# Moving the second batch's first query projection and the first batch's inverse roots in a gated attention and expert kernel

## The reference

```python
x = x + tanh(g_xattn[0]) * xattn(layernorm(x), ctx_2048, Wq, Wk, Wv, Wsk, Wsv, Wo)
x = x + tanh(g_ffn[0]) * ffn(layernorm(x), router, gate, up, down, ...)
```

## Time and profile before

| | |
|---|---|
| median of 3 runs | 894.11 us (891.49 to 894.21) |
| profiled execution | 890.82 us |
| span of the profiled execution | 889.0 us |
| mean granted TensorE clock | 0.994 |
| PE busy | 870.7 us, 98% of the span |
| DVE, POOL, ACT busy | 539.9, 512.7, 398.7 us |

### The profile page before, as it was taken

One profiled execution on the slowest core, in us unless ns is written; L12 is line 12 of the kernel. 1 busy time (PEld: TensorE's weight loads), 2 busy tenths in 40 slices (PEclk: granted clock), 3 DMA queues, 4 the chain that ended last, 5 costly groups with the idle time before them and its releaser, 6 DMA issues.

```text
span 889.0 us, 17360 instructions
## 1 busy us (share of the span) xinstructions
PE 870.7 (98%) x6662; PEld 759.7 (85%) x6662; DVE 539.9 (61%) x977; ACT 398.7 (45%) x806; POOL 512.7 (58%) x532
## 2 busy tenths in 40 slices
PE   8899999999999999899999999999999999999998
PEld 8799999999999998778888867888888888888886
DVE  6566667666666656732246758466565565566567
ACT  5535555454555554654135143443444444444431
POOL 4824343434344322361579995456788888788741
PEclk9989999999999999999999999999999999999999
DMA  8558676767676563880101155402202010121046
GB/s 269 137 165 215 169 195 185 208 167 208 168 208 177 164 177 93 184 289 1 48 25 46 55 167 162 166 24 71 72 25 95 25 71 24 72 72 48 1 134 245
DMA packets 78099, 111.74 MB, mean 126 GB/s; under 512 B 7097, under 2 KB 48826, under 8 KB 76986
## 3 DMA queue, kind: packets, MB, share of 16 engines
q1 hardware_dynamic: 75808, 109.61, 42.2%
q10 hardware_dynamic: 2210, 1.03, 0.5%
HBM read 73.33 MB, written 33.62 MB: 120 GB/s over the span
## 4 chain that ended last, share of the span: by engine, by line
PE 91%; DVE 3%; DMA 2%; POOL 1%; issue 1%; ACT 1%; SPq 0%; POOLq 0%; DVEq 0%
PE ps_scores L2112 20%; PE ps_proj L1763 14%; PE ps_scoresT L2112 10%; PE ps_scoresT L1900 6%; PE ps_scores L1752 6%; PE ps_proj L1752 6%; PE ps_o L1914 6%; PE ps_scores L1873 5%; PE ps_scoresT L1752 5%; PE ps_proj L2112 5%; PE ps_proj L1821 4%; DMA q_kept<-second_qT_hi 1%; DMA xn_rows<-in_x 1%; PE ps_o_max L1932 1%; DVE neg_max L1406 1%
## 5 line engine op out<-in xcount | busy, mean ns | idle before, releaser
L1078 ACT ACTIVATE probsT<-ps_scoresT 128x512 f32<-128x512 f32 (+1 forms) x256 | 138.0, 544 | 148.9 <-PE ps_scoresT L1900 144.8
L1406 DVE TENSOR_REDUCE neg_max<-ps_scores 128x2 f32<-128x384 f32 (+1 forms) x256 | 131.0, 516 | 109.0 <-PE ps_scores L1873 108.3
L1288 ACT ACTIVATE part_sums<-ps_scores 128x512 f32<-128x512 f32 x96 | 57.4, 598 | 133.0 <-PE ps_scores L2112 130.2
L1900 PE MATMUL ps_scoresT<-q_stack,k_stack 116*128 116x256 f32 x448 | 106.3, 309 | 1.7 <-ACT probsT L1078 1.6
L1873 PE MATMUL ps_scores<-k_stack,q_stack 114*128 114x192 f32 (+1 forms) x512 | 96.9, 273 | 8.1 <-DVE neg_max L1406 7.9
L1873 PEld LDWEIGHTS ps_scores<-k_stack,q_stack 114*128 114x128 f32 x512 | 83.0, 194 | 14.8 <-DVE neg_max L1406 8.4
L807 POOL TENSOR_TENSOR o_normal<-o_blocks,inv_sums 128x256 f32<-128x256 f32 x32 | 19.9, 622 | 124.8 <-DVE inv_sums L1427 124.8
L950 POOL TENSOR_TENSOR w_expert_lo<-w_sums,w_expert_hi 128x256 fp32r<-128x256 f32 x64 | 63.8, 1008 | 45.5 <-ACT w_expert_hi L1211 45.5
L962 POOL TENSOR_TENSOR big<-big,basis 128x512 f32<-128x512 f32 x56 | 77.5, 1401 | 15.6 <-DVE basis L1702 15.6
L1900 PEld LDWEIGHTS ps_scoresT<-q_stack,k_stack 116*128 116x128 f32 x448 | 70.0, 190 | 6.3 <-ACT probsT L1078 2.8
L1693 DVE TENSOR_TENSOR basis<-part_sums,silu_gate 128x512 f32<-128x512 f32 x32 | 24.0, 750 | 67.3 <-ACT silu_gate L1296 67.3
(11 more groups left out here) (296 smaller groups left out, 2496.6 us busy)
## 6 DMA issues: line engine op xcount, KB each, us to landing
k_stack<-k_kept SPq DMA_DIRECT2D x64, 192.0 KB, 4.4
q_stack<-q_kept SPq DMA_DIRECT2D x48, 192.0 KB, 4.3
big<-coeff_rows SPq DMA_DIRECT2D x8, 1024.0 KB, 4.7
q_kept<-qT_hi SPq DMA_DIRECT2D x10, 512.0 KB
x_rows<-in_x SPq DMA_DIRECT2D x9, 512.0 KB, 5.4
k_kept<-kT_hi SPq DMA_DIRECT2D x16, 256.0 KB
x_kept<-x_rows SPq DMA_DIRECT2D x16, 256.0 KB, 3.5
w_raw<-in_L_ffn_w_gate SPq DMA_DIRECT2D x16, 256.0 KB, 2.9
```

The costliest lines, as they stand in the source:

```text
L1078: act.activation(PT[:, g % 2, 2 * j:2 * j + blocks].rearrange("p h f r w -> p (h f r w)"), ST[:, n % 2, 0:blocks].rearrange("p h n -> p (h ...
L1288: act.activation(TP[:, u % 2, j, :], src[:, u % 2, :], ACT.Copy).then_inc(taken, 1)
L1406: dve.tensor_reduce(NM[:, g // 2 % 2, g % 2, 2 * i:2 * i + 2], SA[:, n % 2, :, 0:keys], AX.X, ALU.max, negate=True).then_inc(max_done, 1)
L1900: ins = pe.matmul(ST[:, n % 2, v, :], KS[0:ROWS, g, j + v, 1 - v].rearrange("p w s -> p (w s)"), QS[0:ROWS, g, j + v].rearrange("p f r w - ...
```

## The change

Two things are done. First, the query (1, 0): its first half stays in the prologue; the second half of 12 matmuls is cut into four pieces of 3, which go behind the scores of slots 1, 3, 5 and 7. The other three queries of batch 1 move from slots 1 to 14 to slots 9 to 15. Since splitting is tied to the last part, ACT and DVE split the query (1, 0) in slot 8, not in slot 0, and the last of the four in slot 16, not 15; `keep_q(1)` stands in slot 17, not 16, of SP's program.

Second, the inverse roots of batch 0: DVE adds the epsilon (`first_variance`), ACT takes the square root (`first_sqrt`), DVE makes the reciprocal and the Newton step (`first_roots`); POOL no longer does it and starts with `rows_out(1)`. ACT gets two dummy activations of one column (`table_of`) that load the tables of the square root at the start and of the exponential behind the last `rows_out`. DVE splits the weight halves 4 and 5 later, around the normalisation.

```diff
-EARLY_Q = ((-1, -1, -1), (1, 4, 7), (9, 10, 11), (12, 13, 14))
+EARLY_Q = ((-1, -1, 7), (9, 10, 11), (11, 12, 13), (13, 14, 15))
+EARLY_PIECES = {1: 4, 3: 5, 5: 6, 7: 7}
...
         def x_roots(b):
-            pool.wait_ge(stats_done, TB * (b + 1))
+            pool.wait_ge(stats_done, TB * (b + 1) + 1)
             inverse_roots(mv, ve, rstd, tmp, b).then_inc(rstd_done, 1)
...
-        link(pool.memset(half[:], -0.5))
-        x_roots(0)
+        pool.memset(half[:], -0.5).then_inc(ones_set, 1)
+        pool.wait_ge(ones_set, 3)
         rows_out(1)
         x_roots(1)
...
+        def first_sqrt():
+            act.wait_ge(stats_done, TB + 1)
+            act.activation(rstd[:, 0:TB], ve[:, 0:TB], ACT.Sqrt).then_inc(rstd_done, 1)
+
+        def table_of(func):
+            act.activation(tg[:, 0:1], VA[:, 0, 0, 0:1], func)
...
+        act.wait_ge(ones_set, 1)
+        table_of(ACT.Sqrt)
         weights_high(0)
...
-        for n in range(1, 8):
+        for n in range(1, 5):
+            weights_high(n)
+        first_sqrt()
+        for n in range(5, 8):
             weights_high(n)
...
         rows_out(4)
         rows_out(6)
+        table_of(ACT.Exp)
...
+        def first_variance():
+            dve.wait_ge(stats_done, TB)
+            dve.tensor_scalar(ve[:, 0:TB], mv[:, 0:TB, 1], LN_EPS, None, ALU.add).then_inc(stats_done, 1)
+
+        def first_roots():
+            v, r, t = (w[:, 0:TB] for w in (ve, rstd, tmp))
+            dve.wait_ge(rstd_done, 1)
+            link(dve.reciprocal(r, r))
+            link(dve.tensor_tensor(t, r, r, ALU.mult))
+            link(dve.tensor_tensor(t, t, v, ALU.mult))
+            link(dve.tensor_scalar(t, t, -0.5, 1.5, ALU.mult, ALU.add))
+            dve.tensor_tensor(r, r, t, ALU.mult).then_inc(rstd_done, 1)
...
         for t in range(TB):
             row_stats(0, t)
-        for n in range(3, 6):
-            weights_low(n)
+        first_variance()
+        weights_low(3)
+        first_roots()
+        weights_low(4)
         for t in range(TB):
             normalise(0, t)
-        for n in range(6, 8):
+        for n in range(5, 8):
             weights_low(n)
...
         queries(1, 0, 0, 2)
         keys_values("k", 1, 1)
-        queries(1, 0, 1, 2)
         for n in range(SLOTS):
...
+            if n in EARLY_PIECES:
+                queries(1, 0, EARLY_PIECES[n], 8)
             for part in range(3):
...
                 for r in range(G):
                     b = queries_due(n, r, part)
-                    if b is not None:
+                    if b is not None and (b, r) != (1, 0):
                         queries(b, r, part)
```

More of the change, by code:

```diff
@@ L818, in normalise @@
                 n = b * TB + t
-                pool.wait_ge(rstd_done, b + 1)
+                pool.wait_ge(rstd_done, b + 2)
                 pool.tensor_scalar(XN[:, t, :], XN[:, t, :], mv[:, n, 0:1], rstd[:, n:n + 1],
@@ L1352, in normalise @@
             n = b * TB + t
-            dve.wait_ge(rstd_done, b + 1)
-            dve.wait_ge(stats_done, n + 1)
+            dve.wait_ge(rstd_done, b + 2)
+            dve.wait_ge(stats_done, n + 2)
             rows = rows_of(b)[:, t, :]
```

## The result

The changed kernel takes 896.59 us (median of 14 runs, 894.22 to 898.87), the kernel before, run beside it on the same chip, 894.36 us (14 runs, 890.30 to 896.38): ratio 1.0031, 95% interval 1.0015 to 1.0046. It is 0.3% slower. The forecast was 893.8, no change; the range ended at 896.8. The profiled execution took 897.56 us, span 895.5, mean granted clock 0.990 (before: 890.82, 889.0 and 0.994).

A forecast was written before the change was run, and what follows sets the result against it. PE, busy 98%, was taken as the bound, its early stall moving to slot 32 behind SP's queue. Profiled 890.82, minus 1.2 gained, plus 2.6 half clock, gives 892.2; plus 1.6 scatter, 893.8; range 889.3 to 896.8.

The forecast's parts named there:

- The releaser: Sign at slot 32: PE idle for some 6 us up to 72, with DMA `q_stack` as its releaser.
- slot 32, 72.05 predicted: `q_kept` starts at 56.0, plus 16.05 us to land in `q_stack`: slot 32 at 72.05 instead of 73.27, 1.2 gained.
- the 0.3 for the roots: Prologue: moving the inverse roots to DVE and ACT gains 0.2 to 0.3 us for all behind; 0.3 taken.
- The upper bound, 1.0 lost: Roots in the prologue: 1.0 us lost if DVE's new steps are blocked once by a long POOL instruction.
- the half clock behind slot 32: After PE's idle time at slot 32: 5.1 us at half clock, 2.6 lost; bounds nothing to 5.1 lost.
- rival C: Slots 32 to 38: half clock lasts as long as before, 10.24 us; 896.3 to 898 with scatter; chance 0.14.
- A: The forecast: stall moved to slot 32, clock falls there and comes back soon; 892 to 895; chance 0.53.
- Such scatter may come from the front ... I give half of it back: Median stands 3.3 us above the profiled execution; slot 32 swallows earlier scatter, so only 1.6 added: 893.8.
- the row at 15.77: DVE's two subtractions beside POOL's `q_stack` instructions took 1.28, 0.64 each; read as POOL paying, DVE not delayed.
- B's early fall: Rival B, no clock loss at slot 32: clock may fall already between 33.5 and 38.4; 889.6 to 892.9; chance 0.23.
- D's condition: Rival D: `q_kept` issued or landed some 6 us earlier, gain of 7.3 to 7.5 kept; 883.4 to 886; chance 0.05.
- E: Slot 0's stall doesn't go, ACT's table load or another order holding DVE as before; 890.8 to 894; chance 0.05.

The follow-up runs named there:

- e3: Changed kernel with SP's four gates' loads moved behind the write of batch 1's queries (slot 20 instead of 16): 893.96 us, ratio 0.9999.
- e8: Changed kernel with the four loads of Wo moved from slots 24 and 28 to 14 and 15, ahead of the queries' write: 898.94 us, ratio 1.0071.
- e4: Changed kernel with 44 extra matmuls that compute nothing on PE ahead of slot 32's wait for its query stack: 893.84 us, ratio 0.9996.
- e1: Kernel before with the query pieces alone, the roots staying on POOL: 895.70 us, ratio 1.0020.
- e13: Pieces alone on the kernel before, plus the late fill: 892.94 us, ratio 0.9978.
- the late fill: 24 matmuls that compute nothing, spread over slots 230 to 247 of PE; added to the kernel before: 892.06 us, ratio 0.9986.
- e9: Pieces alone; third context load and batch 1's key write issued by ACT instead of SP, gates' loads in slot 20: 890.65 us, ratio 0.9979.
- e2: Changed kernel with the old query order, so the roots alone: 894.18 us, ratio 1.0004.
- e5: Changed kernel with key write and third context load moved forward between batch 0's stacks in SP's queue, gates' loads behind the queries' write: 894.29 us, ratio 1.0024.
- e11: Changed kernel plus the late fill: 893.40 us, ratio 1.0003.
- e15: Changed kernel with SP's key write and context load moved forward and gates' loads later, plus the late fill: 890.89 us, ratio 0.9961.
- e14: Roots alone (changed kernel with the old query order), plus the late fill: 892.91 us, ratio 0.9982.
- e12: Pieces alone with SP's key write and context load moved forward and gates' loads later, plus the late fill: 889.32 us, ratio 0.9956.
- e6: Kernel before with only SP's order changed: key write and third context load moved forward, gates' loads later: 891.35 us, ratio 0.9984.
- e7: Pieces alone, roots on POOL, with SP's key write and context load moved forward and gates' loads later: 890.09 us, ratio 0.9980.

## Why the prediction was wrong, step by step

**Right: the stall and what replaces it.** The wait of 3.97 us went, `second_qT_lo` waits 0.94 us in slot 8 (about 1 predicted), the clock is 1.00 where it was 0.50, slot 18 came 6.7 us earlier (7.5 predicted), PE arrived at slot 32 at 66.87 (65.7) and waited 5.94 (about 6), with a half clock behind. e3, e8 and e4 show the mechanism from both sides.

**The releaser.** The expected DMA `q_stack` stands as "issue" in the row, which names no releaser. That it was the DMA follows from e3 and e8, where slot 32 moves with the write, and from its start 3.1 us behind the issue of the load at 69.75.

**Mis-sized: slot 32, 72.05 predicted, 72.81 measured.** The start of `q_kept` was put at 56.0 (0.6 for SP's wait, 0.3 for the roots) and was 56.91. The 0.6 held; the 0.3 for the roots did not come. DVE goes on from the normalisation 4.20 us after the last aggregate starts, before 4.85, but one weight half of 0.63 that stood ahead of it now follows it; and in this profile the aggregate comes 0.45 later, since the DMA of the rows landed at 9.8 instead of 9.4. SP's first stack load is issued at 28.24 instead of 27.88, and its last gates' load ends at 56.87 instead of 56.26: 0.6 later where 0.3 earlier was counted. These 0.6 us are within the scatter between profiles of one program, so the roots are shown to give nothing here, not to cost it. DVE around the roots, kernel after:

```profile
11.37 0.18 DVE L1365 BATCH_NORM_AGGREGATE mean_var<-stats 128x2 f32<-128x6 f32 x1
11.59 0.19 DVE L1377 TENSOR_SCALAR var_eps<-mean_var 128x2 f32<-128x2 f32 x1
11.69 0.91 DVE L1392 TENSOR_TENSOR wq_lo<-w_stage,wq_hi 128x512 fp32r<-128x512 f32 x1
...
14.42 1.23 DVE L1372 TENSOR_SCALAR xn_rows<-xn_rows,mean_var,rstd 128x512 f32<-128x512 f32 x2
15.57 1.88 DVE L1392 TENSOR_TENSOR wkv_lo<-w_stage,wkv_hi 128x512 fp32r<-128x512 f32 x3
```

The normalisation itself fell from 1.84 to 1.23, as said; the first subtraction took 0.91 instead of 0.64. POOL's cast (10.47 to 11.51) was over by then; its first `q_stack` instruction ran from 11.58. The upper bound, 1.0 lost, did not occur.

**Mis-sized: the half clock behind slot 32.** 5.1 us of it and 2.6 lost were taken; it lasted 3.24 us behind the resumption (72.81 to 76.05), and the marks show 1.2 lost. With 0.1 gained at slot 32, the front is 1.1 us slower; 1.4 was predicted, by two errors that cancel, which is luck. In other kernels of this shape it cost 2.4 or 2.5 (e1, e13), about half of what rival C takes: A and C are one mechanism with a varying length.

**Failed: "Such scatter may come from the front ... I give half of it back".** This is the step that made the forecast wrong. The prediction had found a loss of 1.4 us and then added only 1.6 of the 3.3 us between profile and median, which turned the loss into "no change"; with all 3.3 it would have said 895.5. The profiled execution of before lay 3.5 us under the median of its 14 runs (894.36). It has the front's fall in full (40.31 to 50.55), yet no late one; the late fill takes 2.1 us from the median and more than half of the scatter, and runs with a clock like the profile's are 3.4 us shorter than the others. So most of the 3.5 us are falls that come long after slot 32, which slot 32 cannot swallow; that all of it is, is not shown. PE's waits for the maxima from 350 to 385 us are the same in both kernels, here of before:

```profile
PE ps_scores L1873 <- DVE neg_max L1406: 2.8, 7, 1.1
PE ps_scoresT L1888 <- DVE max_halves L1416: 0.5, 1, 0.5
```

(After has 2.8, 7, 1.1 too, and 0.7 instead of 0.5 in the second row.) The same waits sometimes end in a fall and sometimes not. The whole distance had to be added, not half.

**Missing: 1.0 us in the expert part.** The prediction had no term for it. From the maxima of slot 255 to the end it is 502.8 to 502.9 us in eight of nine profiles without the roots, and 503.7 to 504.2 in eight of nine with them (e9 and e3 are the others). In the kernel after, most of it arises between 555 and 562 us. DVE and POOL there, kernel after:

```profile
556.50 1.82 DVE L1635 TENSOR_TENSOR down_lo<-big,down_hi 128x512 fp32r<-128x512 f32 x1
558.25 1.78 DVE L1682 TENSOR_TENSOR sum_lo<-part_sums,sum_hi 128x512 fp32r<-128x512 f32 x1
...
556.49 1.29 POOL L931 TENSOR_TENSOR part_sums<-xnT_hi,sum_hi 128x512 f32<-128x512 f32 x1
```

PE, kernel after, which from 558.72 to 561.02 had begun a matmul every 0.23 us:

```profile
561.78 0.50 PE L1785 MATMUL ps_proj<-w_down_hi,down_hi 128*128 128x512 f32 x1 [0.37 <-DVE down_lo L1635]
```

DVE and POOL at the same place, kernel before, where PE has no such gap:

```profile
550.84 0.83 DVE L1602 TENSOR_TENSOR down_lo<-big,down_hi 128x512 fp32r<-128x512 f32 x1
551.59 1.77 DVE L1649 TENSOR_TENSOR sum_lo<-part_sums,sum_hi 128x512 fp32r<-128x512 f32 x1
...
551.08 1.74 POOL L930 TENSOR_TENSOR part_sums<-xnT_hi,sum_hi 128x512 f32<-128x512 f32 x1
```

The same subtraction takes 0.83 where it starts 0.24 ahead of POOL's instruction, which then takes 1.74, and 1.82 where it starts 0.01 behind it, which then takes 1.29: whoever comes second pays. The Trainium skill, "SBUF — State Buffer", section "Who interferes with whom", says that two such instructions exclude each other; these rows agree, where the row at 15.77 showed DVE undelayed. This one subtraction takes 1.82 or 1.83 in eight of the 18 profiles (after, e2, e4, e5, e8, e9, e11, e15) and 0.68 to 0.83 in the ten others, and the last `down_lo` of the kernel starts 495.8 to 495.9 us behind the maxima of slot 255 in the eight, 494.9 to 495.0 in the ten. So it happens without the roots too (e9) and not always with them (e3, e14; e14's longer end comes from behind the last `down_lo`). Why the two engines mostly meet in this order with the roots, 540 us behind them, is open.

**The sum as it should have been:** 890.82 + 1.1 (front) + 1.0 (expert part) + 3.5 (from the profile to the median) = 896.4; measured 896.59. The first two terms are of single profiles and the third is of the kernel before, so the close fit is partly luck.

**The rivals.** B's early fall, against which the prediction held that "no stretch of before with that share fell", did not come in the kernel after but came in e1 (36.55 to 39.96), e11 (35.60 to 42.43) and e12 (36.82 to 40.23), in the slots just behind the start; e11's PE still waited 4.9 us at slot 32. D's condition, an earlier `q_kept`, was met by 4.2 us in e3, which kept only 2.4 of it. E did not occur. "Wrong if `q_kept` starts before 55, slot 32 before 70, or PE's idle time is under 3 us": none of these happened, and the forecast of the time was wrong all the same, by terms outside the stretch that they watch.

## What to carry to other kernels

When a stall is removed, follow the work to the next point that another queue feeds, and look there at the order of issue: a queue without gaps takes the whole gain, and moving its order moves the wait to the next load. Before a profiled execution is used as a base, set it against the median of several runs, and look for stretches with small regular waits where the clock falls in some executions; the difference belongs there until something shows otherwise. Where PE must wait, work that computes nothing can be worth its issue: with it slots 32 to 40 took 12.6 us instead of 13.8 here.

## What the runs showed of the hardware

- The clock can be 0.50 without one long idle time ahead: e1 at 36.55, and from between 356 and 361 us in the profiles of after, e1, e2, e3, e5, e8 and e9, where no single wait is over 1.2 us. The four other profiles without the late fill (before, e4, e6, e7) have no fall there. The Trainium skill, "TensorE: Matmul & The Clock Gate", Part 1, has activity release the throttle; nothing here speaks against it, but the waits in these rows do not tell whether the clock falls.
- Behind waits of 2.5 to 7.4 us at slot 32 the stretch at half clock lasted from 3.4 (e9) to 10.2 us (e1, e8, e13); no run tells what sets the length. What it costs goes by the part that lies behind the resumption: 3.2 to 3.7 us of it made slots 32 to 40 longer by 1.2 to 1.5 us (after, e3, e8, e9, e11), 5.3 to 6.2 us by 2.1 to 2.5 (e1, e5, e13, e15).
- A table load amid ACT's work cost its own 1.28 us: `q_stack` ended at 38.97, the load ran from 38.98, the next activation began at 40.28. The drain that the Trainium skill, "ScalarE: Activation LUTs", section "What ACT_TABLE_LOAD costs", adds does not show.
- Three DMAs of 512 KB into DRAM took 12.8 to 13.1 us from first issue to the issue that waited for them in the kernel before, the changed one and e6, and from 12.0 (e8) to 14.7 us (e15) over all 18 profiles, with e3 at 14.55.
